# A decoder layer in one kernel: the mixer's input projection as three fp32r passes, with shared buffers and written-out expert loops

## What is computed

```python
# mixer (x is 16 x 256 x 256, in_w is 512 x 256)
h = x @ in_w.T + in_b
hc = causal_conv(h, conv_w, 4 taps, per channel) + conv_b
h = silu(hc)
xp = h @ xp_w.T + xp_b
a = exp(-exp(xp[..., :16])); b = silu(xp[..., 16:]) * sum(h, -1)
state = state * a_t + b_t            # scan over the 256 tokens
x = layernorm(x + ys @ out_w.T + out_b)
# cross attention: 8 heads of 128, keys and values from the tokens and 77 context rows
x = layernorm(x + attention(x, context) @ Wo + bo)
# mixture of experts: 8 experts, top 2, capacity 512 rows for each
x = layernorm(x + combine(relu(rows @ W1[e]) @ W2[e]))
```

## Time and profile before

| | us |
|---|---|
| median of 3 runs | 1092.27 |
| lowest and highest run | 1091.71, 1095.06 |
| profiled execution, whole | 1085.1 |
| its span, first to last instruction | 1082.9 |
| TensorE matmuls busy | 1000.7 (92%) |
| VectorE, ScalarE, GpSimd busy | 804.7 (74%), 662.5 (61%), 521.6 (48%) |
| TensorE clock granted, mean over the span | 0.969 |

### The profile page before, as it was taken

The page is one execution under the profiler, slowest core; times in us unless marked ns, Lnnn a source line. Parts: engine busy times, 40 slices in busy tenths (PEclk is TensorE's granted clock), DMA queues, the critical chain, the costliest instruction groups (busy, mean ns, idle before and its releaser), DMA issues.

```text
span 1082.9 us, 20863 instructions
## 1 busy us (share of the span) xinstructions
PE 1000.7 (92%) x6878; PEld 935.4 (86%) x6878; DVE 804.7 (74%) x2017; ACT 662.5 (61%) x1714; POOL 521.6 (48%) x830
## 2 busy tenths in 40 slices
PE   5799999999999999999999999999999998299970
PEld 4699999999999999999999999999999898289860
DVE  6877777877787878877887878787878765354526
ACT  5576666666666666666766576657675655145625
POOL 5524353645455545554555354535463534325653
PEclk9899999999999999999999999999999999689985
DMA  7381120112111211122111211121103000575448
GB/s 234 128 245 72 34 95 24 57 33 91 34 51 36 85 42 42 37 72 63 43 37 56 79 42 38 40 94 42 38 17 108 23 33 11 190 230 99 68 49 310
DMA packets 60365, 84.46 MB, mean 78 GB/s; under 512 B 13940, under 2 KB 43688, under 8 KB 60264
## 3 DMA queue, kind: packets, MB, share of 16 engines
q1 hardware_dynamic: 52584, 70.46, 19.5%
q0 software_dynamic: 7680, 12.72, 5.7%
HBM read 44.16 MB, written 38.99 MB: 77 GB/s over the span
## 4 chain that ended last, share of the span: by engine, by line
PE 79%; ACT 8%; DVE 7%; issue 3%; DMA 1%; POOL 1%; ACTq 0%; SPq 0%; DVEq 0%; POOLq 0%
PE ps L563 22%; PE ps L565 21%; PE ps L564 21%; PE ps L590 7%; PE ps L657 3%; PE ps L651 3%; ACT prob L1014 1%; DVE nmx L1431 1%; PE ps L695 1%; ACT fx L1086 1%; DVE cv L1152 1%; ACT k_hi L858 1%; DVE gt L1123 1%; PE ps L681 1%; ACT x2T L912 1%
## 5 line engine op out<-in xcount | busy, mean ns | idle before, releaser
L1639 POOL TENSOR_SCALAR prob<-prob,rinv 128x333 f32<-128x333 f32 x256 | 140.7, 561 | 347.4 <-DVE rinv L1440 346.8
L1009 ACT ACTIVATE oT_hi<-ps 128x256 fp32r<-128x256 f32 x128 | 49.2, 384 | 198.7 <-PE ps L565 198.7
L563 PE MATMUL ps<-kv_lo,w_hi 128*128 128x256 f32 (+1 forms) x512 | 159.0, 310 | 2.9 <-ACT x2T L912 1.0
L565 PE MATMUL ps<-kv_hi,w_hi 128*128 128x256 f32 (+1 forms) x512 | 153.4, 300 | 0.0
L564 PE MATMUL ps<-kv_hi,w_lo 128*128 128x256 f32 (+1 forms) x512 | 153.0, 299 | 0.0
L1014 ACT ACTIVATE prob<-ps,nmx 128x333 f32<-128x333 f32 x256 | 134.7, 536 | 10.5 <-DVE nmx L1431 10.4
L1094 DVE TENSOR_TENSOR pT_lo<-ps,pT_hi 128x512 fp32r<-128x512 f32 (+1 forms) x256 | 130.4, 550 | 0.6 <-ACT pT_hi L1026 0.6
L1431 DVE TENSOR_REDUCE nmx<-ps 128x2 f32<-128x666 f32 x128 | 108.5, 848 | 22.3 <-PE ps L565 21.4
L563 PE MATMUL ps<-pT_lo,v_hi 128*128 128x256 f32 (+1 forms) x384 | 108.5, 282 | 0.9 <-DVE pT_lo L1094 0.9
L590 PE MATMUL ps<-ident,prob 128*128 128x128 f32 (+1 forms) x768 | 107.8, 273 | 1.6 <-DVE oT_lo L1094 1.2
L565 PE MATMUL ps<-pT_hi,v_hi 128*128 128x256 f32 (+1 forms) x384 | 108.3, 282 | 0.0
(11 more groups left out here) (230 smaller groups left out, 3005.7 us busy)
## 6 DMA issues: line engine op xcount, KB each, us to landing
wraw<-in_W SPq DMA_DIRECT2D x14, 512.0 KB, 6.8
vcd_hi<-vst_hi SPq DMA_DIRECT2D x10, 512.0 KB, 2.7
vcd_lo<-vst_lo SPq DMA_DIRECT2D x10, 512.0 KB, 3.6
v_hi<-vcd_hi SPq DMA_DIRECT2D x32, 154.0 KB
v_lo<-vcd_lo SPq DMA_DIRECT2D x32, 154.0 KB
slots<-initr SPq DMA_DIRECT2D x8, 520.0 KB, 7.1
xs<-in_x SPq DMA_DIRECT2D x16, 256.0 KB, 3.8
xts<-in_xT SPq DMA_DIRECT2D x15, 256.0 KB, 3.5
```

The lines of the kernel that those rows point to most:

```text
L563: pe.matmul(dst, hi1, lo2, start=first, stop=False, skip_group_check=True)
L565: return pe.matmul(dst, hi1, hi2, start=False, stop=last, skip_group_check=True)
L1009: act.activation(oT_hi[:, h % 2, :], ps[:, AVB, 0:S], ACT.Copy).then_inc(oTh_set, 1)
L1639: pool.tensor_scalar(prob[:, h % 2, t, 0:KEYS], prob[:, h % 2, t, 0:KEYS], rinv[:, h % 2, t:t + 1], 1.0, ALU.mult, ALU.mult).then_inc(norm ...
```

## The change

1. Unit `in` of batches 3 to 15 runs `three` on high and low parts: twelve fp32r matmuls for each half in place of four float32 ones. Batches 0 to 2 stay as they were.
2. The weights' parts `inw_hi`, `inw_lo` are made once, in body 0: ScalarE in slot 3, GpSimd in slot 4. The input's parts `xt_hi`, `xt_lo` are made in each body from 1 to 13: ScalarE at the end of slot 1, GpSimd in slot 2 behind the probabilities.
3. Room: the weights' parts lie where `raw` is, the input's parts where `initr` (zeros that clear the slots) and `xrow_b` (last batch's rows) are. So expert 0's weights are loaded in body 14 and not in body 0.
4. SyncE's wait before `xts`: from body 2 on for the input's low part instead of for TensorE.
5. The hardware loops of TensorE's and GpSimd's experts are written out, `need_apart` is `need` everywhere, four semaphores of the last stage's loads are reused.

```diff
-        raw = sb("raw", [P, 2, 1024])
+        rawbuf = ExitStack()
+        raw = sb("raw", [P, 2, 1024], F32, rawbuf)
+        rawbuf.close()
+        inw_hi = sb("inw_hi", [P, KD, DI], F32R)
+        inw_lo = sb("inw_lo", [P, KD, DI], F32R)
...
-        initr = s1("initr", [P, ST, ROW])
+        clear = ExitStack()
+        initr = sb("initr", [P, ST, ROW], F32, clear)
+        clear.close()
+        lastrow = ExitStack()
+        xrow_b = sb("xrow_b", [P, NT, ROW], F32, lastrow)
+        lastrow.close()
+        xt_hi = s1("xt_hi", [P, KD, S], F32R)
+        xt_lo = s1("xt_lo", [P, KD, S], F32R)
...
                 if "aft" in have:
-                    need_apart(sp, in_mm, 2 * (b + 2))
+                    sp.wait_ge(in_mm, min(2 * (b + 2), 6))
+                    need(sp, xTl_set, b - 1)
                     sp.dma_start(xts[:], xT_d[bass.ds(b + 2, 1)].rearrange("o p k s -> (o p) k s")).then_inc(xT_ld, 16)
...
-                if at(b, 0):
-                    sp.wait_ge(wk_lo_set, 4)
-                    sp.wait_ge(cvec_mm, 1)
+                if at(b, B - 2):
+                    sp.wait_ge(in_mm, 2 * B)
                     sp.dma_start(w1r, W1[0]).then_inc(w1r_ld, 16)
                     sp.dma_start(w2r, W2[0]).then_inc(w2r_ld, 16)
...
-                if name == "in":
+                if name == "in" and bb > 2:
+                    pe.wait_ge(inw_parts, 2)
+                    pe.wait_ge(xTl_set, bb - 2)
+                    for c in range(2):
+                        o = slice((2 * idx + c) * P, (2 * idx + c + 1) * P)
+                        for k in range(KD):
+                            last = three(g[:, c * S:(c + 1) * S], inw_hi[:, k, o], inw_lo[:, k, o],
+                                         xt_hi[:, k, :], xt_lo[:, k, :], k == 0, k == KD - 1)
+                    last.then_inc(in_mm, 1)
+                if name == "in" and bb < 3:
...
-            with pe.Fori(1, E // 2) as i:
-
-                inner(2 * i - 1, 1)
-                rows(2 * i, 0, 16 * i)
-                outer(2 * i - 1, 1)
-                inner(2 * i, 0)
-                rows(2 * i + 1, 1, 16 * i + 16)
-                outer(2 * i, 0)
+            for e in range(1, E - 1):
+                u = e % 2
+                inner(e, u)
+                rows(e + 1, 1 - u, 16 * ((e + 1) // 2 + (1 - u)))
+                outer(e, u)
...
+            def rows_hi(bb):
+
+                act.wait_ge(xT_ld, 16 * bb)
+                act.wait_ge(in_mm, 2 * bb)
+                act.wait_ge(init_st, 16 * (E + 1))
+                act.activation(xt_hi[:], xts[:], ACT.Copy).then_inc(xTh_set, 1)
...
+                    if at(b, 0) and h == 3:
+                        act.wait_ge(wk_lo_set, 4)
+                        act.wait_ge(cvec_mm, 1)
+                        act.activation(inw_hi[:], inw[:], ACT.Copy).then_inc(inw_parts, 1)
+                    if h == 1 and "aft" in have and b:
+                        rows_hi(b + 2)
...
+                    if at(b, 0) and h == 4:
+                        pool.wait_ge(inw_parts, 1)
+                        pool.tensor_tensor(inw_lo[:], inw[:], ap(inw_hi[:]), ALU.subtract).then_inc(inw_parts, 1)
+                    if h == 2 and "aft" in have and b:
+                        pool.wait_ge(xTh_set, b)
+                        pool.tensor_tensor(xt_lo[:], xts[:], ap(xt_hi[:]), ALU.subtract).then_inc(xTl_set, 1)
...
-            with pool.Fori(1, E // 2) as i:
-                add(2 * i - 1, 1)
-                add(2 * i, 0)
-            add(E - 1, 1)
+            for e in range(1, E):
+                add(e, e % 2)
```

More of the change, by code:

```diff
@@ L315, in build @@
             sem("fnm_set"), sem("fy_set"), sem("out_st"))
-        def need_apart(eng, sem, value):
-            need(eng, sem, value)
-            if not isinstance(value, int):
-                eng.sem_inc(passed, 1)
         def freed(name, idx, b):
@@ L421, in next_context @@
             def next_context(c):
-                need_apart(sp, cxn_set, c)
+                need(sp, cxn_set, c)
                 sp.dma_start(cxs[:], ctxt[bass.ds(c, 1)].rearrange("o p d -> (o p) d")).then_inc(ctx_ld, 16)
@@ L428, in keep_context @@
                 need(sp, cxl_set, c + 1)
-                need_apart(sp, cx_st, 32 * c)
+                need(sp, cx_st, 32 * c)
                 for d, part in zip(cx_tiles, (cx_hi, cx_lo)):
@@ L435, in keep_values @@
                 need(sp, vcl_set, 2 * c + 2)
-                need_apart(sp, vc_st, 32 * c)
+                need(sp, vc_st, 32 * c)
                 for d, part in zip(vc_tiles, (vst_hi, vst_lo)):
@@ L499, in body @@
                 if "att" in have:
-                    need_apart(sp, av_mm, 8 * b)
+                    need(sp, av_mm, 8 * b)
                     values(b, 1)
@@ L505, in body @@
                 if "nxt" in have:
-                    need_apart(sp, cx_st, 32 * tile + 32)
-                    need_apart(sp, k_mm, 8 * b)
+                    need(sp, cx_st, 32 * tile + 32)
+                    need(sp, k_mm, 8 * b)
                     for d, part in zip(cx_rows, (kv_hi[1 - par], kv_lo[1 - par])):
@@ L513, in body @@
                 if "nxt" in have:
-                    need_apart(sp, vc_st, 32 * tile + 32)
-                    need_apart(sp, av_mm, 8 * b + 4)
+                    need(sp, vc_st, 32 * tile + 32)
+                    need(sp, av_mm, 8 * b + 4)
                     values(a, 0)
@@ L1129, in unit @@
                     need(dve, slot_set, bb)
-                    need_apart(dve, dots_mm, bb + 1)
+                    need(dve, dots_mm, bb + 1)
                     for t in range(NT):
@@ L1133, in unit @@
                     for t in range(NT):
-                        need_apart(dve, m8_set, 2 * bb + t + 1)
+                        need(dve, m8_set, 2 * bb + t + 1)
                         dve.max_index(i8[:, t, :], m8[:, t, :], g[:, t * E:(t + 1) * E]).then_inc(i8_set, 1)
@@ L1176, in context_stats @@
                 dve.bn_stats(x_st[:], cxs[:]).then_inc(xstat_set, 1)
-                need_apart(dve, xstat_set, 3 * c + 1)
+                need(dve, xstat_set, 3 * c + 1)
                 dve.bn_aggr(x_mv[:], x_st[:]).then_inc(xstat_set, 1)
@@ L1218, in mixed @@
                 for t in range(NT):
-                    need_apart(dve, astat_set, 6 * a + t + 1)
+                    need(dve, astat_set, 6 * a + t + 1)
                     dve.bn_aggr(a_mv[:, t, :], a_st[:, t, :]).then_inc(astat_set, 1)
@@ L1254, in residual_stats @@
                 for t in range(NT):
-                    need_apart(dve, cstat_set, 5 * b - 4 + t)
+                    need(dve, cstat_set, 5 * b - 4 + t)
                     dve.bn_aggr(c_mv[:, t, :], c_st[:, t, :]).then_inc(cstat_set, 1)
@@ L1560, in context_norm @@
                 need(pool, ctx_mm, c)
-                need_apart(pool, xrs_set, c + 1)
+                need(pool, xrs_set, c + 1)
                 pool.tensor_scalar(cxn[:], cxs[:], x_mv[:, 0:1], x_rs[:], ALU.subtract,
@@ L1579, in latents_part @@
                 need(pool, lnf_set, 2 * b + 3)
-                need_apart(pool, k_mm, 8 * b)
+                need(pool, k_mm, 8 * b)
                 pool.tensor_copy(kv_hi[1 - par][:, 0, 0:S], full[:, 0, 0:S]).then_inc(kvh_set[0], 1)
@@ L1588, in normalised @@
                 a = b + 1
-                need_apart(pool, ars_set, a + 1)
+                need(pool, ars_set, a + 1)
                 for t in range(NT):
@@ L1636, in body @@
                     if "att" in have:
-                        need_apart(pool, rinv_set, n + 1)
+                        need(pool, rinv_set, n + 1)
                         for t in range(NT):
@@ L1648, in body @@
                         need(pool, sc_done, 64 * (b - 1))
-                        need_apart(pool, crs_set, b)
+                        need(pool, crs_set, b)
                         for t in range(NT):
@@ L1680, in body @@
                                            ).then_inc(route_step, 1)
[L1681 removed]
+                        need(pool, route_step, r + 3)
                         pool.tensor_tensor(tot[:], mask[:, :, 0, :], mask[:, :, 1, :], ALU.add).then_inc(tot_set, 1)
@@ L1723, in add @@
                 for s in range(ST):
-                    need_apart(pool, yo_set, 4 * e + s + 1)
+                    need(pool, yo_set, 4 * e + s + 1)
                     pool.indirect_dma_start(accd, bass.IndirectOffsetOnAxis(tku[u][:, s:s + 1], 0), yo[u][:, s, :],
```

22 lines of the change are left out of this document (11 added, 11 removed).

## The result

The changed kernel takes 1089.01 us in the median of six runs (1087.95 to 1089.92), the kernel before beside it 1092.08 us (1091.71 to 1095.20). The ratio is 0.9956, with a 95% interval of 0.9939 to 0.9973: faster by 0.44%, just beyond the 0.3% that a measurement tells. The medians alone are 3.1 us apart (0.28%), the means 4.1 us; how large the gain is stays uncertain by a microsecond or two, that there is one does not. The prediction was 1088.5 us.

A forecast was written before the change was run, and what follows sets the result against it. TensorE, 92% busy, was taken to bound the kernel, saving time only where its next step is ready: 13 x 0.30 = -3.9 us in slot 6, +0.1 in body 0, so 1092.27 becomes 1088.5 us; range 1084.0 to 1093.0 us.

The forecast's parts named there:

- Price of the unit: Unit `in` on TensorE: 0.30 us shorter, 2.39 to 2.09 us with its transposes, read from unit `q`.
- The quarter: Unit `in` by the skill's rule, three passes as three quarters of four: 0.43 us off a unit, -5.6 us in sum.
- the +0.1 of the other terms: Body 0's making of the weights' parts, once: 0 to +1.1 us, taken as +0.1 us.
- Slot 6 pays all: Half of `in` in slot 6: the whole 0.30 us becomes time in 13 bodies, -3.9 us.
- Slot 4 pays nothing: Half of `in` in slot 4: nothing gained, since `op` waits for `k_lo` of key head 5.
- The splits, zero: Input's parts on ScalarE and GpSimd: hidden in idle time, 1.5 and 3.4 us to spare; 0, at most +0.1 us a body.
- nothing pays: Rival: slot 6's 0.30 us becomes a wait elsewhere or the unit runs no faster; 1092.3 us, chance 0.14.
- Body 0, +0.1: Weights' parts made on ScalarE in slot 3 and GpSimd in slot 4 of body 0: +0.1 us, once.
- Loads and loops, zero: Expert 0's loads moved to body 14, SyncE's new wait, and the experts' loops written out: each 0.
- rival of code supply in the experts: Rival: instruction fetches come late in the experts' straight code, 7.3 us if one is exposed; 1095.8 us, chance 0.04.
- The step from 1085.1 to 1092.3 us: Profiled execution against median shown, 7.2 us: nothing in the change touches what makes them differ, so carried over.
- Clock, no change: TensorE's granted clock: stays as it was, since TensorE stays as full and body 14's idle time left its slice at 9 or more.

The follow-up runs named there:

- e8_two_passes: Changed kernel without the product of the weights' low part and the input's high part, eight matmuls a unit for twelve: 1086.77 us, ratio 0.9926.
- e3_only_slot6: Changed kernel with three passes only for the half of `in` in slot 6, float32 again in slot 4: 1083.01 us, ratio 0.9954.
- e4_only_slot4: Changed kernel with three passes only for the half of `in` in slot 4, float32 again in slot 6: 1088.33 us, ratio 0.9998.
- the reordering: Kernel before with slot 4's order changed: `k_hi`, `k_lo` ahead of the state's parts, `x2T`'s copy ahead of `pT_hi`; 1086.25 us, ratio 0.9923.
- e7_loops_kept: Changed kernel with the hardware loops of TensorE's and GpSimd's experts put back: 1089.11 us, ratio 0.9952.
- e1_before: The kernel before, unchanged, on the first chip: 1088.41 us, ratio 1.0003.
- e2_after: The changed kernel, unchanged, on the first chip: 1084.49 us, ratio 0.9958 to the kernel before.

## Why the prediction was right

**The forecast's mechanism holds**: 0.44% of 1092.1 us is 4.8 us by the ratio and 3.1 us between the medians; -3.8 was forecast, and the slots of the first chip say -3.5. That the absolute figure came within 0.5 us is in part luck, for it hangs on the chip: the changed kernel takes 1084.5 us on the first and 1089.7 on the third.

- *Price of the unit, 0.30 us.* Measured 2.39 - 2.07 = 0.32. It came from `q`, the same instruction at the same kind of place. The quarter that the Trainium skill's four passes would give (FP8 and Floating Point Precision, TensorE Precision Notes), 0.43 us a unit, did not come: `e8_two_passes` has a pass at 0.118 us, where a quarter of 0.43 us would be 0.108. A float32 matmul's 0.43 us would fit four passes of 0.108, but an fp32r pass costs more than that. (With the +0.1 of the other terms the sum by this rule is -5.5, not -5.6.)
- *Slot 6 pays all.* 102.1 to 98.1 us, -4.0 against -3.9; `e3_only_slot6` has the whole gain.
- *Slot 4 pays nothing.* Right: 121.6 and 121.7 us, and `e4_only_slot4` at 0.9998. Body 14, which had no unit `in` and takes 52.5 us where bodies 1 to 13 take 53.7 or 56.7, was the natural experiment. But the reason given was only half: I named the chain to `k_lo` and missed that `q`, the unit behind `op`, was held a second time by the copy of `x2T`. It made no difference to the number, since both holds lie off TensorE. By the timelines it is why the reordering gained 0.6 us and not 0.2.
- *The splits, zero.* ScalarE's remaining idle time 1.57 us (1.5 forecast), GpSimd's 3.44 (3.4). Not forecast: slot 7 is longer by 0.1 to 0.2 us over fourteen bodies, and by 0.7 more in `e8_two_passes`. It is a small piece of the rival "nothing pays": there VectorE's `oT_lo` comes later in slot 7. What the 0.1 to 0.2 us of the changed kernel wait for is open.
- *Body 0, +0.1.* Not testable: body 0 takes 57.6, 55.1 and 57.9 us in three traces of the kernel before, 57.5, 58.3 and 57.5 in three of the changed one.
- *Loads and loops, zero.* Shown by `e4_only_slot4` and `e7_loops_kept`. The rival of code supply in the experts fell with their times, 97.2 to 98.6 us in the five traces with the loops and 98.0 to 98.6 in the nine of straight code, and with the 0.11 us between expert 2 and 3.
- *The step from 1085.1 to 1092.3 us.* The prediction carried these 7.2 us over as something that the change doesn't touch. That was right and matters most. The late `q_hi` costs 5.6 to 7.0 us in slot 1 over bodies 3 to 14; the profiled execution before didn't have it, the changed kernel's has it. The kernel before takes 1088.0 us on the chip without it and 1095.1 on the third, with it. So it probably makes up most of the 7.2 us, though none of the kernel before's slower executions that were timed beside the result left a trace. Had I set the two spans side by side, I would have read 4.1 us slower.
- *Clock, no change.* Right for the changed kernel: both pages have the same digits up to the end of the batches. (They begin 9, 8, 9, so the second slice, which the prediction called full, is not. Nothing hangs on it.) But body 14's idle time is not safe: in two of fourteen traces, `e4_only_slot4` and `e8_two_passes`, the clock fell behind it, which cost 1.5 us each.

Of the expectations behind the prediction, that of `e8_two_passes` was missed in the median, as told there, and two failed on one point: that once slot 4's chain was shortened, the float32 unit would become the bound. It ends in time for the shortened chain, so the three passes of slot 4 are worth nothing that these runs can tell in either order.

**Open:** why the completion of `q` reaches ScalarE late in every trace of the second and third chip and in none of the first. TensorE's starts are the same in both cases. GpSimd issues four indirect DMAs to `slots` in just that stretch (432.49 to 437.83 us in the changed kernel's body 7), but it does so on the first chip as well, at the same distance. The packets of these DMAs take as long in either case (0.13 us in the mean). Moving them was not tried.

The recording of the traces is a rival that no run tests. The nine traces with the late `q_hi` hold 10098 to 10145 semaphore increments, the five without it 10847 to 10869. What is missing is nearly all from slot 0, from 2 to 7 us after its first scores, in bodies 2 to 15: the stretch of the same DMAs and of the late `q`. So either the recording delays TensorE's signals there, or one cause does both. Every timed run here has a span and a clock from such a recording, so the two can't be told apart. What is said of the change does not hang on it, since each ratio compares kernels on one chip.

## What to carry to other kernels

On an engine that is 92% busy, ask of each unit separately whether the engine waits behind it: half of this change was worth 0.4%, the other half nothing. Where it does wait, look at what stands ahead of the awaited step in the queues of the other engines; exchanging three steps there won 0.77% with no work removed. And before two traces are compared by their spans, cut both into slots: a difference in a slot that the change doesn't touch belongs to the chip until the kernel before, run beside it, says otherwise.

## What the runs showed of the hardware

- A matmul's completion can reach the waiting engine more than a microsecond late: in body 7 of the changed kernel's first trace `q_hi` starts 437.55 - 435.88 = 1.67 us after the last matmul of `q`, where the same matmul stands at 435.12 in `e1_before` and `q_hi` follows after 0.32 us. The gap it left on ScalarE was mostly near 0.6 or near 1.3 us, in every body from 3 to 14, on some chips and not on others, with the same program. The semaphore's increment is itself late (1.64 us after the matmul's start, else 0.30), and so is that of the next unit, `v` (1.16 us, else 0.41), while the matmuls go on at their usual distances. Traces with this delay lack some 700 of 10850 semaphore increments, so it may come from the recording.
- An idle time of TensorE of 1.68 us was followed by a granted clock of 0.61 over 4.3 us in one trace, and by full clock in others with an idle time as long (1.67 us in `e2_after`).
- One fp32r pass over 256 columns costs 0.118 us, a float32 matmul of the same size 0.43 us: three passes save 18% of it, at a granted clock of 1.00.
